# A decoder layer whose attention and expert phases become one program per engine, with the expert weights split in the attention's drain and small products on PE that nobody reads

## The reference

```python
x = layernorm(x + attn(x))            # 16 heads of width 16, one shared key and value head
x = layernorm(x + xattn(x, context))  # 120 context rows, queries and keys through two linear maps, a mask
x = layernorm(x + ffn(x))             # 8 experts, top 2 of a softmax gate
# ffn, for each expert e and each token:
#   h = x @ W1[e].T + b1[e];  a, b = split(h);  out += ((a * sigmoid(b)) @ Wo.T + bo) * comb[e]
```

## Time and profile before

| | |
|---|---|
| median of three runs | 1470.23 us |
| the profiled execution's own time | 1475.48 us |
| its span, first to last instruction | 1472.9 us |
| mean granted clock of PE | 0.952 |
| busy: PE, DVE, ACT, POOL | 1276.2, 1136.1, 755.9, 656.9 us |
| instructions | 29966 |

### The profile page before, as it was taken

How to read it: one execution, slowest core, us unless ns; L and a number is a source line. 1 busy time by engine, 2 the same in 40 slices (tenths; PEclk the granted TensorE clock), 3 DMA queues, 4 the chain that set the end, 5 groups by cost and what they waited for, 6 DMA issues and landing times. The chain is left out here.

```text
span 1472.9 us, 29966 instructions
## 1 busy us (share of the span) xinstructions
PE 1276.2 (87%) x7668; PEld 899.1 (61%) x7669; DVE 1136.1 (77%) x3110; ACT 755.9 (51%) x1743; POOL 656.9 (45%) x1018
## 2 busy tenths in 40 slices
PE   6888999999999999999987307999999999968886
PEld 4443555555555555555544206888888888858876
DVE  1455788888888888888864387888888888859998
ACT  1125677777777777777775242223223322314444
POOL 1011244454544444545444472343334333447886
PEclk9998999999999999999997558999999999989999
DMA  4436456656646656655636522334433443369995
GB/s 101 106 61 101 80 104 132 127 117 133 122 120 128 128 116 122 129 120 117 122 107 234 197 81 84 130 130 133 137 131 130 133 137 130 130 247 322 336 334 198
DMA packets 171822, 211.67 MB, mean 144 GB/s; under 512 B 20048, under 2 KB 143056, under 8 KB 167632
## 3 DMA queue, kind: packets, MB, share of 16 engines
q1 hardware_dynamic: 147808, 143.92, 40.9%
q0 software_dynamic: 17680, 55.28, 10.1%
q10 hardware_dynamic: 6240, 11.34, 2.2%
HBM read 124.81 MB, written 84.89 MB: 142 GB/s over the span
## 5 line engine op out<-in xcount | busy, mean ns | idle before, releaser
L853 DVE TENSOR_REDUCE negmax<-psS 128x2 f32<-128x512 f32 x512 | 349.2, 686 | 100.1 <-PE psS L625 94.4
L755 ACT ACTIVATE probs<-psT 128x512 f32<-128x512 f32 x512 | 303.4, 598 | 171.7 <-PE psT L635 165.1
L1331 ACT ACTIVATE sig<-hb 128x512 f32<-128x512 f32 x136 | 86.1, 633 | 286.9 <-DVE hb L1414 279.8
L625 PE MATMUL psS<-kstack,qstack 96*128 96x256 bf16 x1024 | 195.4, 273 | 33.8 <-DVE kstack L949 15.3
L635 PE MATMUL psT<-qstack,kstack 99*128 99x512 bf16 x512 | 194.9, 382 | 5.1 <-ACT probs L755 5.1
L1211 POOL DMA_INDIRECT g_rows<-g,slot x136 | 135.6, 997 | 70.7 <-issue 67.4
L625 PEld LDWEIGHTS psS<-kstack,qstack 96*128 96x128 bf16 x1024 | 92.4, 104 | 90.7 <-DVE negmax L853 34.8
L391 POOL DMA_INDIRECT lists<-x,slots x128 | 127.0, 992 | 34.2 <-issue 30.3
L523 PE MATMUL psO<-probs,vaug 128*32 128x512 f32 x1024 | 140.4, 621 | 0.9 <-ACT probs L755 0.8
L1425 DVE SCALAR_TENSOR_TENSOR g<-g,xe,sig 128x512 f32<-128x512 f32 x136 | 102.2, 751 | 28.5 <-DVE g L1421 16.8
L1414 DVE TENSOR_TENSOR hb<-psHb,f_b 128x512 f32<-128x512 f32 x136 | 94.0, 691 | 37.5 <-issue 34.7
(11 more groups left out here) (201 smaller groups left out, 2950.7 us busy)
## 6 DMA issues: line engine op xcount, KB each, us to landing
rows<-g_rows SPq DMA_DIRECT2D x32, 1024.0 KB, 8.0
qstack<-q_parts SPq DMA_DIRECT2D x192, 128.0 KB
xe<-lists SPq DMA_DIRECT2D x136, 133.0 KB, 2.1
q_parts<-qpart SPq DMA_DIRECT2D x32, 384.0 KB, 2.8
sums<-x SPq DMA_DIRECT2D x32, 264.0 KB, 2.3
x2in<-sums SPq DMA_DIRECT2D x32, 264.0 KB, 4.7
xt<-in_x_t SPq DMA_DIRECT2D x32, 256.0 KB, 6.0
xres<-in_x SPq DMA_DIRECT2D x32, 256.0 KB, 3.2
```

Of the source, the lines that this page charges most:

```text
L625: last = mm(psS[:, u % 2, hh * S:(hh + 1) * S], qstack[0:KROWS, b1.s4, 2 * hp + hh, c * P:(c + 1) * P], kstack[0:KROWS, b1.s4, :], start=T ...
L755: nc.scalar.activation(probs[:, u % PT, :], psT[:, u % 2, :], ACT.Exp, scale=SELF_SCALE).then_inc(sm["exp_done"], 1)
L853: v.tensor_reduce(negmax[:, b1.s2, 2 * hp:2 * hp + 2, c], psS[:, u % 2, :].rearrange("p (h k) -> p h k", h=2), AX.X, ALU.max, negate=True) ...
```

## The change

Both phases now return functions instead of opening blocks, and one block calls them one after the other on each engine. Memory is placed anew so that the experts' tensors lie over what the attention no longer needs. ACT casts the first weights in steps B+3 to B+5, DVE makes six of the eight differences in steps B+4 and B+5, and POOL makes none. The biases and Wo are loaded in step B+4. Pad rows are made and stored to HBM in step 0, and SP copies them behind the lists, from HBM to HBM. The tables are made with whole-table operations. PE makes four products of 128 columns in each unit of the steps B+3 to B+5 and 80 after them; nobody reads them. The diff, cut to its core:

```diff
+W1_ORDER = (4, 5, 6, 7, 0, 1, 2, 3)
+def split_w1(ops, eng, dram, nth):
+    part = dram["piece"](W1_ORDER[nth])
+    eng.wait_ge(dram["w1_rounded"], nth + 1)
+    ops.tensor_tensor(dram["w1_lo"][:, part], dram["w1_raw"][:, part], dram["w1_hi"][:, part].bitcast(F32), ALU.subtract
+                      ).then_inc(dram["w1_split"], 1)
 ...
         def load_experts(t):
-            if t.n == B + 1:
-                (bo and the eight b1 pieces)
             if t.n == B + 3:
                 wait(sp, "pv_done", 4 * B)
                 wait(sp, "exp_done", UNITS * B)
                 for e in range(E):
-                    sp.dma_start(dram["w1_raw"][:, :, e * H2:(e + 1) * H2],
+                    sp.dma_start(dram["w1_raw"][:, dram["piece"](e)].rearrange("p (c h) -> p c h", c=DC),
                                  io["f1_t"][e].rearrange("(c p) h -> p c h", p=P)
                                  ).then_inc(dram["w1_loaded"][e], 16)
+            if t.n == B + 4:
+                wait(sp, "cross_scored", B)
+                wait(sp, "mask_ready", B)
+                (bo)
+                wait(sp, "score_link", B)
+                (wo_raw, then the eight b1 pieces)
 ...
+        def expert_constants():        # POOL, in step 0 behind the split of the queries
+            pool.memset(pad[:, :, :], 0.0).then_inc(sm["pool_chain"], 1)
+            (listbase, number, upper, the ids of the pad rows)
+            pool.dma_start(dram["pad_rows"].rearrange("(k p) r -> p k r", p=P), pad[:, 0:E, :]
+                           ).then_inc(dram["pads_stored"], 16)
+            pool.dma_start(dram["lists"][E * STRIDE:E * STRIDE + E * P, :].rearrange("(k p) r -> p k r", p=P),
+                           pad[:, E:, :]).then_inc(dram["pads_stored"], 16)
 ...
+        def keep_warm(count):          # PE
+            for _ in range(count):
+                mm(psS[:, 0, 0:P], all_ones[:, :], before[:, :], start=True, stop=True)
             for u in range(UNITS):
+                if B + 3 <= t.n < B + 6:
+                    keep_warm(4)
 ...
+            if t.n == B + 5:
+                keep_warm(80)
 ...
+        def round_w1(e):               # ACT, at the end of the unit
+            act.wait_ge(dram["w1_loaded"][e], 16)
+            if e == 4:
+                act.wait_ge(dram["pads_stored"], 32)
+            if e == 0:
+                wait(act, "cross_scored", B)
+                wait(act, "mask_ready", B)
+            copy(dram["w1_hi"][:, dram["piece"](e)], dram["w1_raw"][:, dram["piece"](e)]
+                 ).then_inc(dram["w1_rounded"], 1)
+        rounds = {(B + 3, 15): W1_ORDER[0:2], (B + 4, 0): W1_ORDER[2:3], (B + 4, 7): W1_ORDER[3:4],
+                  (B + 4, 12): W1_ORDER[4:6], (B + 5, 7): W1_ORDER[6:7], (B + 5, 12): W1_ORDER[7:8]}
 ...
+        splits = {(B + 4, 3): 2, (B + 4, 6): 1, (B + 5, 3): 3}      # DVE, at the end of the unit
+                for _ in range(splits.get((t.n, u), 0)):
+                    split_w1(v, dve, dram, halved)
+                    halved += 1
 ...
+    def sync(sp, drained):             # experts, SP
+        sp.wait_ge(dram["pads_stored"], 32)
+        sp.wait_ge(sm["pads_placed"], 1)
+        for e in range(E):
+            row = sp.value_load(pad_tab[0:1, e:e + 1], min_val=0, max_val=(E - 1) * STRIDE + T)
+            sp.dma_start(dram["lists"][bass.ds(row, P), :], dram["pad_rows"][e * P:(e + 1) * P, :]
+                         ).then_inc(sm["pads_written"], 16)
+        drained(sp)                    # x2_stored and dispatched of the last batches
+        sp.wait_ge(sm["tables_ready"], 2)
+        sp.wait_ge(sm["pads_written"], 16 * E)
 ...
+        def expert(w, e, first):       # PE, in place of a slice over columns e * H2 + first
+            return lambda k: w[:, bass.ds(e * (DC * H2) + (k * H2 + first), H)]
 ...
+    def tensor(pe):
+        pe.wait_ge(sm["tables_ready"], 2)
+        pe.wait_ge(dram["w1_split"], E)
+        (wo_split is waited for ahead of the first product with Wo)
 ...
+    def vector(dve, halved):
+        v.tensor_copy(pad_tab[:, :], last).then_inc(sm["pads_placed"], 1)
         link(v.tensor_tensor(cnt[:, :], last, listbase[:, :], ALU.subtract))
         link(v.tensor_scalar(cnti[:, :], cnt[:, :], float(P - 1), None, ALU.add))
         link(v.tensor_single_scalar(cnti[:, :], cnti[:, :], 7, ALU.logical_shift_right))
         link(v.tensor_copy(ntile[:, :], cnti[:, :]))
+        link(v.tensor_tensor(below[:, :, :], upper[:, :, :], ntile[:, :].unsqueeze(1).to_broadcast([P, E, E]), ALU.mult))
+        v.tensor_scalar(skip[:, :], ntile[:, :], -float(P), float(STRIDE), ALU.mult, ALU.add)
+        link(v.tensor_reduce(upto[:, :], below[:, :, :], AX.X, ALU.add))
+        link(v.tensor_tensor(past[:, :, :], (number over E), (upto over TILES), ALU.is_ge))
+        link(v.tensor_tensor(past_skip[:, :, :], past[:, :, :], (skip over TILES), ALU.mult))
+        link(v.tensor_reduce(rowf[:, :], past_skip[:, :, :], AX.X, ALU.add))
+        link(v.scalar_tensor_tensor(rowf[:, :], number[:, :], float(P), rowf[:, :], ALU.mult, ALU.add))
         v.tensor_scalar(row_tab[:, :], ...).then_inc(sm["tables_ready"], 1)
+        link(v.tensor_reduce(expf[:, :], past[:, :, :], AX.X, ALU.add))
         v.tensor_scalar(exp_tab[:, :], ...).then_inc(sm["tables_ready"], 1)
+        for nth in range(halved, E):
+            split_w1(v, dve, dram, nth)
+        dve.wait_ge(dram["wo_rounded"], 1)
+        v.tensor_tensor(wo_lo[:, :, :], wo_raw[:, :, :], wo_hi[:, :, :].bitcast(F32), ALU.subtract
+                        ).then_inc(dram["wo_split"], 1)
 ...
+        @block.tensor                  # and the same for the other four
+        def _(pe):
+            first["tensor"](pe)
+            second["tensor"](pe)
```

More of the change, by code:

```diff
@@ L94, in sem @@
     def sem(name):
-        return ctx.enter_context(nc.semaphore(name))
+        return dram["semaphores"].enter_context(nc.semaphore(name))
+    base, ident, neg_half, neg_one, eps_c = (dram[k] for k in ("base", "ident", "neg_half", "neg_one", "eps_c"))
+    ROW = D + E + 2
+    keymap = sb("keymap", [P, DC, B * SC])
+    keybias = sb("keybias", [P, B * SC])
+    wq = sb("wq", [P, DC, D])
+    wk = sb("wk", [P, DC, KROWS])
+    wv = sb("wv", [P, DC, DK])
+    kstack = sb("kstack", [P, 4, S], BF16)
+    att = sb("att", [P, 2, QC, D])
+    xres = sb("xres", [P, 2, QC, D])
+    att_t = sb("att_t", [P, 2, 2 * S])
+    vaug = sb("vaug", [P, 4, QC, 32])
+    ksmall = sb("ksmall", [P, 2, S], BF16)
+    uvec_all = sb("uvec_all", [P, DC, P])
+    rden = sb("rden", [P, 2, QC * 8])
+    with nc.sbuf_tensor("pad", [P, 2 * E, ROW], F32) as pad:
+        pass
+    sb("w1_hi_high", [P, dram["w1_piece"] * E // 2])
     qstack = sb("qstack", [P, 4, NH, S], BF16)
@@ L1310, in _, with scalar @@
         pair_pipeline(pe, pair_step)
-    @block.scalar
-    def _(act):
+    def scalar(act):
         copy = nc.scalar.copy
-        act.wait_ge(sm["wo_loaded"], 16)
-        copy(wo_hi[:, :, :], wo_raw[:, :, :]).then_inc(sm["wo_rounded"], 1)
-        for e in range(E):
-            act.wait_ge(dram["w1_loaded"][e], 16)
-            copy(w1_hi[:, :, e * H2:(e + 1) * H2], w1_raw[:, :, e * H2:(e + 1) * H2]).then_inc(sm["w1_rounded"], 1)
+        act.wait_ge(dram["wo_loaded"], 16)
+        copy(wo_hi[:, :, :], wo_raw[:, :, :]).then_inc(dram["wo_rounded"], 1)
         def step(t):
@@ L1493, in decoder_layer @@
             "stride": stride,
             "out": out,
-        }
-        with nc.sbuf_tensor("w1_raw", [P, D // P, E * H2], F32) as w1_raw:
-            dram["w1_raw"] = w1_raw
-        for phase in (attention, experts):
-            with ExitStack() as own:
-                phase(nc, own, io, dram)
+            "semaphores": ctx,
+            "w1_piece": D // P * H2,
+            "piece": lambda e: slice(e * (D // P) * H2, (e + 1) * (D // P) * H2),
+        }
+        DC, H, QC, W1 = D // P, H2 // 2, 2, E * (D // P) * H2
@@ new lines, in decoder_layer, with place @@
+        dram["w1_loaded"] = [ctx.enter_context(nc.semaphore(f"w1_loaded{e}")) for e in range(E)]
+        with ExitStack() as late:
+            def place(name, shape, dt=F32):
+                dram[name] = late.enter_context(nc.sbuf_tensor(name, shape, dt))
+            place("b1", [P, E * H2])
+            place("bo", [P, D])
+            with nc.sbuf_tensor("result", [P, 4, QC, D], F32) as result:
+                dram["result"] = result
+            place("w1_hi", [P, W1], F32R)
+            with nc.sbuf_tensor("w1_raw", [P, W1], F32) as w1_raw:
+                dram["w1_raw"] = w1_raw
+            with (nc.sbuf_tensor("rows", [P, 4, QC, 2 * H], F32) as rows, nc.sbuf_tensor("row_sum", [P, 4, H], F32) as row_sum,
+                  nc.sbuf_tensor("x2in", [P, 4, QC, D + E], F32) as x2in, nc.sbuf_tensor("y", [P, 4, QC, D], F32) as y):
+                dram.update(rows=rows, row_sum=row_sum, x2in=x2in, y=y)
+            place("w1_lo", [P, W1], F32R)
+            second = experts(nc, late, io, dram)
```

(23 more changed lines are left out.)

222 lines of the change are left out of this document (76 added, 146 removed).

## The result

The kernel after takes **1451.09 us** (median of four runs, 1448.31 to 1452.7); the kernel before, run beside it, 1471.58 (1467.3 to 1477.19). The ratio is 0.9857, 95% interval [0.9819, 0.9894]: about 20.5 us, 1.4%. The forecast was 1445.1, range 1431 to 1457. The profiled execution took 1448.31 us, against 1475.48.

The account below looks back on a forecast made before the run. PE bounds both phases, so only the hole between them can go: T 12.3 us later, first expert product at T+15.4, hence -25.1 us. From 1475.48 that gives 1450.4, less 5.25 to the median 1445.1; range 1431 to 1457.

Parts of the forecast that it names:

- The hole: Stretch between attention and expert phase where PE has no matmul, 836.5 to 890.9 us; claimed as what the change can remove.
- (a): End of step B+3: ACT's casts wait for late weight pieces ahead of the norm; +8.1 us, bounds 0 to +10.
- The rival that nothing in the drain is late: Six weight pieces land before ACT asks, so (a) falls away and (c) is 5.4; 1439 us, chance 0.20.
- (c): Three DVE splits behind the last variance hold up POOL's four small instructions; +3.5 us, bounds 1.6 to 5.4.
- (b): Step B+4: ACT's next cast sits between norm and copy, partly hidden by PE's transposes; +0.7 us.
- (d): Small products on PE in the drain: +1.9 us at half clock, -2.2 at full; taken as 0.
- T: End of attention's last DVE step, 838.12 us in the kernel before; forecast to move by 12.3 us to 850.4.
- DVE after T: DVE's work behind attention: short table instructions and four larger operations, tables at T+7.9, two splits done at T+12.5.
- SP decides: After T, SP's eight pad DMAs, 1.12 us apart, and first xe load set the first expert product at T+15.4.
- dear pads: Rival: SP's pad register loads and DMAs cost twice 1.12 us each; +9 us, 1454 us, chance 0.12.
- rivals 1 and 2: Nothing in the drain is late (0.20), and small products hold the clock (0.14); each 1439 us, both together 1435.
- the third rival: Expert loop: addressing or weight placement lengthens PE's products; 15 ns each cancels the gain, 30 gives 1494 us; chance 0.06.

Follow-up runs that it names:

- e1: Kernel after, with SP loading the eight weight pieces in the order in which ACT casts them; 1444.66 us.
- e6: Kernel after, with loads in cast order, pad rows over two queues, and DVE's splits placed so that they don't run beside POOL's chain; 1441.0 us.
- e10: Kernel after, with all of ACT's casts behind attention's last step and all of DVE's splits behind the tables; 1446.88 us.
- e11: e6 with a sixth split in the drain, at unit 11 of step B+4; 1435.3 us.
- e3: Kernel after, with the three DVE splits of step B+5 moved behind the tables; 1444.87 us, one run.
- e8: Kernel after, with 220 instead of 80 small products at PE's end of attention; 1452.34 us.
- e5: Kernel after, with four of the eight pad loads and DMAs issued by ACT and four by SP; 1447.29 us.
- e7: Kernel after, with the expert's weights addressed as [expert, rest], so the register's part is the same for all products of a tile; 1451.27 us.
- e9: Kernel after, with all eight DVE splits behind the tables and ACT's casts left in the drain; 1452.12 us.
- e4: Kernel before, with the three POOL splits moved to DVE, so all eight run there; 1455.88 us, one run.

## Why the prediction was right, and where its terms were off

- **The bound.** The hole was what could be had, and it went from 54.4 us to 17. Shown.
- **(a) ACT waits for the pieces: +8.1 forecast.** From SP's issue to the norm of step B+4 it was 15.4 us and is 23.4: +8.0. e1 takes the wait away, and 7.0 us with it. Shown. The rival that nothing in the drain is late is out. That the two figures meet so closely is in part luck: in the four traces of the new program that do without this wait (e1, e6, e10, e11) the norm comes 13.6 to 13.8 us after the issue, and the 15.4 are from one trace, at a granted clock of 0.69 in the 10 us after the issue, where after and e1 have 1.00.
- **(c) three splits in front of POOL's chain: +3.5 forecast, +5.4 measured**, the upper bound. The step that was mis-sized is "I take 3.5, the middle": the casts, late as in (a), were ready before the splits all the same, and each POOL instruction met one. e3 shows it (1.4 us for the chain with no split near), and e6 that the place of the splits decides: it has two at the same step, behind POOL's chain, and the chain takes 1.4 us. By the Trainium skill, SBUF — State Buffer, section "SBUF: two separate sides", a DVE instruction with two SBUF inputs and a GpSimd (POOL) instruction that reads SBUF exclude each other. By that rule the upper bound holds wherever splits are ready, and the traces of after (6.85 us) and e3 (1.4 us) agree.
- **(b), (d) the third cast and the small products: +0.7 and 0 forecast**, +1.0 together (14.4 less 8.0 and 5.4), which is within the 3 us by which single traces differ; neither is shown apart. Without small products T moves by 0.4. In e8 the granted clock is 1.00 while the products run and 0.50 in the first tile. By the Trainium skill, TensorE: Matmul & The Clock Gate, section "Why this matters for your kernels", idle gaps between bursts bring the clock down; the trace of e8 agrees, with a gap of 4.8 us.
- **DVE after T.** Tables T+7.9 forecast, T+7.5 measured; splits T+12.5 and T+11.9. No instruction over 1.3 us but the splits. Shown.
- **SP decides: T+15.4 forecast, T+15.8 measured.** The pads are 1.32 us apart, not 1.12, which is +1.4; from the last pad to the first `xe` it took 1.0 less, so that the two errors nearly cancel. e5 shows that the pads decide; of the rival's 9 us for dear pads 1.4 are real. The dispatches, put at T+8.5, land at T+9.9 in e5; behind eight pads this is hidden, behind four it is what SP waits for.
- **The sum.** T moved by 14.4, not 12.3, and SP took 0.4 more: from issue to the first transpose -22.6, where -25.1 was forecast. With the 2.0 us of the next point this is the 4.6 us by which 20.5 falls short of 25.1. In the working itself, three roundings: SP's terms add to 15.3, the chances of the four cases to 0.88, and rivals 1 and 2 together without (c) give 1429, just outside the stated range.
- **The per-tile time, taken at nothing: +2.0 us.** First and last transpose of the loop, before and then after:

```profile
890.90 0.66 PE L1272 MATMUL psX<-ident,xe 128*128 128x128 f32 x2 [54.40 <-DVE w_lo L1126]
...
1296.94 0.38 PE L1272 MATMUL psX<-ident,xe 128*128 128x128 f32 x2
```

```profile
1270.03 0.38 PE L1282 MATMUL psX<-ident,xe 128*128 128x128 f32 x2
```

406.04 us became 408.04 (from 861.99). Leaving out the first two intervals and a few disturbed ones, a tile takes 3.005 us in both kernels of the old layout and 3.020 to 3.021 us in all eleven traces of the new: the third rival is real, at 1.3 ns a product where 15 would have eaten the gain. That these 2.0 us were put at nothing is the other term that failed, next to (c). e7 doesn't find the cause; other places of the weights and of the constants in SBUF were not tried: open.
- **Edits at nothing** (POOL's constants at step 0, the biases in step B+4) stayed at nothing: POOL is busy 11.1 us in the first 40 in place of 4.6, and no engine waits for it.
- **-6.3 us of early arrival at the issue** were in no term. They made the profiled run look 26 us faster. As the issue comes anywhere from 786.4 to 802.3 us in traces of both kernels, I take them for scatter.

## What to carry to other kernels

Work put into an engine's idle time is free only if nothing behind it in that queue, and nothing on an engine that stalls beside it, is on the chain: here it cost 15.9 us of attention to save 9.5 (the casts lost, the splits gained: e9), and most of the same work placed behind the waits that free it, with loads in the order of use and the pads over two queues, started the experts 14 to 15 us sooner than the kernel after (e6, e11). When a move takes one cost away, list who is second and third: behind the pads stood the dispatches and the splits within 3 us. Compare stages from an event that both traces have, since two spans can differ by 6 us before the change begins to act, and take a second trace of the same code to learn how far one stage scatters (55.0 and 57.9 us here).

## What the runs showed of the hardware

- A small POOL instruction beside DVE splits of 128x2048 took 1.59 to 2.65 us in place of 0.19 to 0.72; in e3, with no split near, the three from `nmean` on took 1.3 us, not 6.7. Both directions occur: POOL's splits held one DVE comparison for 14.01 us, and without them none took over 0.50 (e4).
- Eight loads of 1 MB issued within 7.2 us landed 6.9 to 21.5 us after issue. Moving the fifth to the front of the order was worth 7.0 us to the engine that waits for it (e1).
- A register load with a DMA behind it took 1.3 us a pair on SP, and the same on ACT (four in 4.57 us).
- After 12 us of small products at full clock, 4.8 us of idle PE were followed by half clock in the first tile (e8). Whether products that reach right up to it would keep the clock was not tried.
- With the same code on PE the clock rose at 823.5 us in one trace and at 828.5 in another, and the drain was 55.0 and 57.9 us long (after, e7).
- With twelve products of the same shapes and four register instructions of either kind per tile, a tile takes 15 ns more in the new program than in the old (3.020 against 3.005 us), in all eleven traces of the one and both of the other. The cause is open.
